# A four-layer graph network on one core: the sage layer of one graph beside the second layer's sums of the next

## Time and profile before

| | us |
|---|---|
| median of 3 runs | 9451.15 |
| the profiled execution | 9428.1 |
| its span | 9426.5 |
| busy in it: PE / DVE / ACT / POOL | 5518.7 / 6030.4 / 4617.4 / 5142.9 |
| mean granted TensorE clock | 0.796 |

### The profile page before, as it was taken

How to read it: one execution, slowest core, us unless ns; L and a number is a source line. 1 busy time by engine, 2 the same in 40 slices (tenths; PEclk the granted TensorE clock), 3 DMA queues, 4 the chain that set the end, 5 groups by cost and what they waited for, 6 DMA issues and landing times.

```text
span 9426.5 us, 190384 instructions
## 1 busy us (share of the span) xinstructions
PE 5518.7 (59%) x62584; PEld 4902.9 (52%) x62584; DVE 6030.4 (64%) x7458; ACT 4617.4 (49%) x4674; POOL 5142.9 (55%) x5234
## 2 busy tenths in 40 slices
PE   3673771266765567466775667564774668563036
PEld 2663771254765467364764557463773548462025
DVE  5874872276866677586866777585875768573024
ACT  5643740355726466265735566254744567261034
POOL 0004777677727676276726774276744777176720
PEclk9886885688888789787887889787886789786568
DMA  2114332334313523234313432125322343223210
GB/s 95 42 33 108 71 69 31 55 79 93 74 47 61 121 58 77 51 65 108 67 45 73 116 65 68 46 47 130 60 59 62 85 84 73 65 42 72 26 22 28
DMA packets 305351, 629.20 MB, mean 67 GB/s; under 512 B 113273, under 2 KB 163962, under 8 KB 268666
## 3 DMA queue, kind: packets, MB, share of 16 engines
q0 software_dynamic: 91936, 161.87, 16.1%
q1 hardware_dynamic: 207922, 456.31, 13.8%
q10 hardware_dynamic: 4752, 0.14, 0.0%
HBM read 506.89 MB, written 111.15 MB: 66 GB/s over the span
## 4 chain that ended last, share of the span: by engine, by line
DVE 28%; PE 22%; issue 13%; ACT 7%; POOL 4%; DVEq 3%; DMA 2%; ACTq 2%; POOLq 0%; SPq 0%
PE ps L1318 6%; DVE keys L1063 4%; PE ps L1293 3%; PE ps L1320 3%; PE ps L1343 3%; DVE key L1053 3%; ACT Pbuf L690 3%; PE ps L1274 2%; PE ps L1271 2%; ACT Hn L690 2%; PE ps L1367 2%; DVE Hn L923 2%; DMA G<-table,idx 2%; DVE key L1039 2%; DVE Zs L943 1%
## 5 line engine op out<-in xcount | busy, mean ns | idle before, releaser
L541 POOL DMA_INDIRECT G<-table,idx x1416 | 1502.3, 1061 | 510.0 <-issue 448.9
L1320 PE MATMUL ps<-Hn,AT 128*128 128x99 bf16 x12288 | 1763.4, 216 | 0.0
L533 POOL DMA_DIRECT2D idx<-lists x433 | 260.0, 600 | 2731.1 <-issue 2246.7
L1320 PE MATMUL ps<-X,AT 128*128 128x99 bf16 x12288 | 1739.9, 215 | 0.0
L690 ACT ACTIVATE Hn<-Rb,q 128x2048 int8<-128x2048 f32 x768 | 1484.1, 1987 | 66.9 <-PE ps L1320 63.9
L690 ACT ACTIVATE Pbuf<-Rb,q 128x2048 int8<-128x2048 f32 x768 | 1487.2, 1987 | 17.7 <-PE ps L1320 15.4
L541 POOL DMA_INDIRECT best<-table,idx x1024 | 1102.7, 1077 | 321.8 <-issue 309.4
L1318 PE MATMUL ps<-X,Hn 128*128 128x198 bf16 x6144 | 939.5, 269 | 554.1 <-DVE Hn L923 304.2
L1320 PEld LDWEIGHTS ps<-Hn,AT 128*128 128x128 fp8e4 x12288 | 1252.1, 102 | 0.0
L1320 PEld LDWEIGHTS ps<-X,AT 128*128 128x128 fp8e4 x12288 | 1245.9, 101 | 0.0
L1318 PE MATMUL ps<-Hn 128*128 128x198 bf16 x6144 | 950.5, 270 | 430.8 <-DVE Zs L943 241.5
(11 more groups left out here) (186 smaller groups left out, 11651.5 us busy)
## 6 DMA issues: line engine op xcount, KB each, us to landing
Rb<-in_adj SPq DMA_DIRECT2D x128, 1024.0 KB
Rb<-rrows SPq DMA_DIRECT2D x104, 1024.0 KB, 6.4
bytes_A<-A SPq DMA_DIRECT2D x128, 256.0 KB
bytes_AT<-AT SPq DMA_DIRECT2D x128, 256.0 KB
AT<-bytes_AT SPq DMA_DIRECT2D x128, 256.0 KB, 3.4
AT<-bytes_A SPq DMA_DIRECT2D x128, 256.0 KB, 3.4
G<-table,idx POOLq DMA_INDIRECT x1416
h<-Hn SPq DMA_DIRECT2D x16, 1024.0 KB, 4.2
```

The costliest lines, as they stand in the source:

```text
L533: pool.dma_start(idx[:, slot, :], lists[bass.ds(r, 1)].rearrange("o p k -> (o p) k")).then_inc(idx_in[slot], 16)
L541: pool.indirect_dma_start(out=dst[:, k, :], out_offset=None, in_=table, in_offset=bass.IndirectOffsetOnAxis(ap=idx[:, slot, k:k + 1], axis ...
L1320: ins = pe.matmul(both[:, 0, 0:G], A8[:, jb, at], v[:, 0:G], start=False, stop=jb == T - 1, skip_group_check=True)
```

## The change

The sage layer of graph b moves from behind LB of graph b+1 to beside its sums. TensorE works on it after a key block's matmuls: after block 1 it waits for gather b and for h1, x1; after blocks 1 to 8 it transposes two tiles into bank 6, after blocks 2 to 9 it does the products of two tiles into bank 7. ScalarE copies a pair of tiles at once and does norms 4 and 2 ahead of LB's Exp and norm 1. VectorE adds the bias to pair p after weighing block p+4 and takes its statistics after block p+5; gamma, beta, relu, the sum into X2 and statistics 2 (`joined`) stand between the last block and `finish`. The three parts of tile 8's list stand after blocks 0, 1 and 2, and SyncE stores them. E of `finish` and WH of LC move to other places of their buffers. For graph 0's LB there is nothing beside, and the last graph's sage layer runs alone.

```diff
             load(0, True)
-            first(0, True)
+            heads_of(0, True)
+            beside(0, None)
...
                 with eng.Fori(0, B - 2) as b:
-                    second(b, False)
+                    beside(b + 1, b)
+                    middle(b, False)
                     last_layer(b, b + 2, False)
-                    first(b + 2, False)
+                    heads_of(b + 2, False)
...
# SyncE, beside
+            def beside(b, other):
+                if b is None:
+                    restore(other + 1, other)
+                    return
                 exponentials(LB, 1, b)
                 sp.dma_start(Rb[:, 0, :], rrows[1, 0, :].partition_broadcast(P)).then_inc(S[LB]["rin0"], 16)
+                if other is not None:
+                    store_lists(b, LIST_LB)
...
# ScalarE
+            def sage_operands(b):
+                s = M["sage"]
+                with act.Fori(0, T // 2) as tt:
+                    plain(act)
+                    act.wait_ge(s["T"], b * T + tt * 2 + 2)
+                    act.wait_ge(s["W"], b * T + tt * 2 + 2)
+                    act.activation(hT[:, :, :, :], ps[:, 6, :].rearrange("p (u k c) -> p u k c", u=2, k=2),
+                                   ACT.Copy).then_inc(s["hT"], 2)
...
+            def beside(b, other):
+                if b is not None:
+                    prepare(LB, b)
+                if other is not None:
+                    sage_operands(other)
+                    norm(4, other, Y, Y, ACT.Identity)
+                    norm(2, other, X2, Hn2, ACT.Relu)
+                if b is not None:
+                    elu_exp(LB, b, 0)
+                    norm(1, b, X, Hn, ACT.Relu)
...
# VectorE
+            def sage_sums(b, p):
+                plain(dve)
+                dve.wait_ge(M["sage"]["W"], b * T + (2 * p + 4))
+                dve.tensor_tensor(Y[:, 2 * p:2 * p + 2, :], ps[:, 7, 0:2 * F].rearrange("p (t f) -> p t f", t=2),
+                                  rowsb[:, 0:1, :].broadcast_to([P, 2, F]), ALU.add).then_inc(M["sage"]["ev"], 2)
+            def sage_statistics(b, p):
+                plain(dve)
+                dve.wait_ge(M["sage"]["ev"], b * T + (2 * p + 4))
+                for t in (2 * p, 2 * p + 1):
+                    dve.bn_stats(stats[:, t, :], Y[:, t, :]).then_inc(ln[4]["st"], 1)
+            def beside(b, other):
+                rest_of = []
+                between = [] if other is None or b is None else list(zip((0, 1, 2), list_tile(b, LIST_LB)))
+                if other is not None:
+                    for p in range(T // 2):
+                        between.append((p + 4, lambda p=p: sage_sums(other, p)))
+                        between.append((p + 5, lambda p=p: sage_statistics(other, p)))
+                    between.append((T // 2 + 4, lambda: rest_of.append(deviations(4, other))))
+                    between.append((T // 2 + 5, lambda: rest_of[0]()))
...
+                    prepare(LB, b)
+                    weigh(LB, 0, (b + 1) * 16, slice(0, 1), b, between)
+                if other is not None:
+                    joined(other)
+                if b is not None:
+                    finish(LB, b, lone)
+                    statistics(1, b, X)
...
# TensorE
+            def sage_step(b, jb):
+                if jb == 1:
+                    sage_arrived(b)
+                if 2 <= jb < T // 2 + 2:
+                    sage_product(b, jb - 2)
+                if 1 <= jb < T // 2 + 1:
+                    sage_turned(b, jb - 1)
...
+            def sums(L, hn, other):
...
                     ins.then_inc(s["pe"], 1)
+                    if other is not None:
+                        sage_step(other, jb)
```

More of the change, by code:

```diff
@@ L385, in load, with heads_of @@
                         sp.dma_start(stage_i32[:, u, :], src).then_inc(adj_in[u], 16)
-            def first(b, alone):
+            def heads_of(b, alone):
                 plain(sp)
@@ L455, in restore, with middle @@
                 sp.dma_start(flat(X2), of(x1, after - 1)).then_inc(x1_in, 16)
-            def second(b, alone):
-                if alone:
-                    restore(b + 1, b)
+            def middle(b, alone):
                 with sp.Fori(0, T) as t:
@@ L489, in _ @@
             sp.sem_inc(out_done, 16)
-            pipeline(sp, load, first, second, last_layer)
+            pipeline(sp, load, heads_of, beside, middle, last_layer)
             sp.wait_ge(out_done, B * 16 + 16)
@@ L814, in _ @@
             act.wait_ge(ready, 1)
-            pipeline(act, load, first, second, last_layer)
+            pipeline(act, load, heads_of, beside, middle, last_layer)
         @block.vector
@@ L825, in statistics, with moments, deviations @@
                                  src[:, bass.ds(t, 1), :].rearrange("p o c -> p (o c)")).then_inc(ln[k]["st"], 1)
+                moments(k, b)
+            def moments(k, b):
+                deviations(k, b)()
+            def deviations(k, b):
                 plain(dve)
@@ L834, in statistics, with inverse @@
                 v(dve.tensor_tensor(small[:, 4, :], small[:, 4, :], small[:, 3, :], ALU.add))
[L836 to L840, removed]
+                def inverse():
+                    plain(dve)
+                    dve.wait_ge(ln[k]["root"], b + 1)
+                    v(dve.reciprocal(small[:, 0, :], small[:, 4, :]))
+                    v(dve.scalar_tensor_tensor(small[:, 1, :], small[:, 2, :], -0.5, small[:, 0, :], ALU.mult, ALU.mult))
+                    v.end()
+                return inverse
             def prepare(L, b):
@@ L885, in weigh @@
             def weigh(L, slot, loaded, h, hn, between=()):
-                after = dict(between)
                 s = S[L]
@@ L896, in weigh @@
                                              ALU.max, ALU.mult).then_inc(s["p"], 1)
-                    if jb in after:
-                        after[jb]()
+                    for at, work in between:
+                        if at == jb:
+                            work()
             def split(L, m, h, u, k):
@@ L1161, in first @@
                 heads(LA, b, lone, (b, *(LIST_ALL if alone else LIST_LA)))
[L1162 to L1176, removed]
-                plain(dve)
-                dve.wait_ge(M["sage"]["ev"], (b + 1) * T + 2)
-                statistics(4, b, Y)
+            def sage_sums(b, p):
+                plain(dve)
+                dve.wait_ge(M["sage"]["W"], b * T + (2 * p + 4))
+                dve.tensor_tensor(Y[:, 2 * p:2 * p + 2, :], ps[:, 7, 0:2 * F].rearrange("p (t f) -> p t f", t=2),
+                                  rowsb[:, 0:1, :].broadcast_to([P, 2, F]), ALU.add).then_inc(M["sage"]["ev"], 2)
@@ new lines, in sage_statistics @@
+            def sage_statistics(b, p):
[12 more added lines that the diff above has]
+                    between.append((T // 2 + 5, lambda: rest_of[0]()))
+                if b is None:
+                    for at, work in sorted(between, key=lambda part: part[0]):
+                        work()
+                else:
+                    prepare(LB, b)
[5 more added lines that the diff above has]
+                    statistics(1, b, X)
@@ L1180, in second, with joined @@
+            def joined(b):
                 v = Chain(dve, M["sage"]["y"], b * 3, 3)
@@ L1237, in last_layer, with prepare @@
                 dve.tensor_tensor(X2[:, :, :], X2[:, :, :], Y, ALU.add).then_inc(x_done, 1)
-            pipeline(dve, load, first, second, last_layer)
+            pipeline(dve, load, heads_of, beside, middle, last_layer)
         @block.tensor
         def _(pe):
-            def prepare(L, b, source, arrived):
+            def prepare(L, b, source, arrived, alone=False):
                 s, w = S[L], Wf[L]
                 W = L.H * L.D + 2 * L.H
-                if not arrived:
+                if L is LB:
                     plain(pe)
                     pe.wait_ge(S[LA]["pv"], ((b + 1) * LA.H + 2) * POST[LA])
+                if L is LC:
+                    plain(pe)
+                    pe.wait_ge(S[LB]["pv"], (b + (2 if alone else 3)) * POST[LB] + 3)
                 for tt in range(T // 2):
@@ L1282, in prepare, with sage_turned, sage_product, sage_arrived @@
                 pe.matmul(ps[:, 6, 0:L.H * L.C], ones[:, :], hpart[:, 0:L.H * L.C], start=True, stop=True).then_inc(s["hs"], 1)
-            def sums(L, hn):
+            def sage_turned(b, p):
+                s = M["sage"]
+                plain(pe)
+                pe.wait_ge(s["hT"], b * T + (2 * p + 2))
+                for u in range(2):
+                    pe.transpose(ps[:, 6, 2 * u * P:(2 * u + 1) * P], Hn2[:, 2 * p + u, :], ident[:, :])
+                    ins = pe.transpose(ps[:, 6, (2 * u + 1) * P:(2 * u + 2) * P], Agg[:, 2 * p + u, :], ident[:, :])
+                ins.then_inc(s["T"], 2)
+            def sage_product(b, p):
+                s = M["sage"]
+                plain(pe)
+                pe.wait_ge(s["hT"], b * T + (2 * p + 4))
```

(24 more changed lines are left out.)

18 lines of the change are left out of this document (10 added, 8 removed).

## The result

The changed kernel takes 9320.38 us (median of 4 runs, 9293.71 to 9324.41) against 9456.33 for the kernel before in the same comparison: ratio 0.9855, 95% interval [0.9833, 0.9877], 136 us less. Two later comparisons gave 0.9841 [0.9819, 0.9863] and 0.9853 [0.9827, 0.9879]. The direction was right, but the gain is nearly double the 72 us that I had forecast, and 9320 lies under my range (9335 to 9450). The profiled execution took 9293.71 (span 9292.0), 134 us under the one before.

A forecast was written before the change was run, and what follows sets the result against it. No engine binds; order and waits set the time. Terms +58 + 189 - 323 + 13 = -63, gather 7 -4, tail about -5: together -72, so 9451 - 72 = 9379 us (profiled execution 9356), range 9335 to 9450.

The forecast's parts named there:

- Rivals 1: Gathers take 2% longer beside denser work, 18 us each, replacing the sage layer as bound: 9435 us, no change; chance 0.14.
- rival 2: Sums of seven LB stages: TensorE's clock stays 0.50 through blocks 3 to 9, +206 us, 9585, slower; chance 0.10.
- the list's pause: TensorE stands still after blocks 0 to 2 for tile 8's list; some 8 us with two rounds, clock loss +2.5.
- Rival 3: More hidden than counted: LB stages grow by 22 us each, checked by gathers 1, 5 and 6: 9346 us; chance 0.14.
- Graph 0: Graph 1's LB stops after block 1 until gather 0 ends at 1741.1; LC(0)'s first hT copy at 1861: +58 us.
- Six LB stages: Graphs 2 to 7, first weighing to LC: three stages at 30.1 and three at 32.8 us longer, +189 us.
- a wait of +13: Graph 3's LB, block 1: TensorE waits 20 us for gather 2, hiding the list's pause and clock loss; +13 remain.
- Gather 7: Last gather: follows norm 1 of graph 7 by 12.0 instead of 16.4 us, -4, and takes 828.4 us again.
- My Theory A: Rerun's forecast: gather 0 933 us as VectorE stands still, gather 7 815 as sage 6 leaves its first tiles.
- The removed stretches, 5 x 64.6: Passes of LC(1) to LC(5): LC's first hT copy follows norm 1 at once, 64.6 us less each, -323 us.
- the tail: After gather 7: the last sage layer stands alone with its statistics between the pairs, about -5 us.

The follow-up runs named there:

- the wait alone: The kernel before with one edit: TensorE waits after key block 1 of LB for the gather of the graph before; 9528.5 us, ratio 1.009.
- second and third executions: The changed kernel run again twice, unchanged, in the first and the last of three comparisons; medians 9303.3 and 9303.2 us.
- late `joined`: The changed kernel with `joined` behind statistics 1 and norm 2 behind norm 1 in every LB with a sage layer; run twice, 9275.5 and 9270.2 us.
- the kernel with its loop turned round: The changed kernel with graph 0's sage layer alone after gather 0, not beside graph 1's LB, which turned the loop's order round; 9325.6 us, ratio 0.986.

## Why the prediction was off

Its mechanism held step by step. LC's first copy follows norm 1 within 0.1 us. From the first weighing, the last one ended after 71.5 to 74.0 us (one round) and 79.2 to 81.8 (two) against 73 and 81.2 forecast, and `finish` began after 90.9 to 93.5 and 98.5 to 101.1 against 93.6 and 101.6. TensorE stood 320.6 us at gather 0 (340 forecast) and met gather 2, for which I had forecast 20 us, and gather 5, which I had given 5 us of room. Gather 1 started at 1853 (1873 forecast), gather 7 at 8094 (8145). Rivals 1 and 2 did not occur: gathers 0 and 7 became shorter, not 2% longer, and the pace of the blocks was 4.9 us. In graph 5's pass the granted clock was 0.50 in the list's pause (5863.6 to 5873.8) and 1.00 from 5874 to 5930, with TensorE busy 53.2 of 56 us. What I took from the Trainium skill for rival 2 stands on its page "TensorE: Matmul & The Clock Gate" under "A second HAM failure mode: psum-queue depth-cycling", right behind the section that I named; these rows hold no such short stops and do not test it. Rival 3 had the direction, but for another reason: the LB stages grew by 24.9 to 32.8 us each, not by its 22, so that its 9346 lies nearer to the result is luck. By the profiled execution three terms of the sum were mis-sized, and one held:

- **Graph 0: forecast +58, measured +38** (1841.3 against 1803.1; 1838 and 1840 in the other two executions). 14 of the 20 are gather 0's end. I took its length as given, "everything up to the end of gather 0" outside the edit, while the edit empties VectorE beside it. This is the step that failed in kind, and the wait alone showed it. In the prediction I had written down that GpSimd stretches VectorE's small steps, and did not turn the sentence round.
- **Six LB stages: forecast +189 and a wait of +13, measured +168 together.** The waits for gathers 2 and 5 (7.6 and 5.9 us) hid in the list's pause and cost 1 to 3. The five stages inside the loop took 3 to 6 us less than forecast each, the last one, outside it, 3 more. Most of this lies between `finish` and norm 1's end, 35.6 us for a forecast 38.1: the table load that I put before the Exp fell beside VectorE's steps (L677 at 5949.32), and the next one, for norm 1's Sqrt, ran ahead of its wait instead of behind it (L630 at 5952.54), so that statistics 1 and norm 1 took 17.8 us for 19.6. In the last LB both loads stood behind their waits, and statistics 1 and norm 1 took 19.9. Up to the last weighing the pace of the steps (4.9 us for 5.07) gave some 1 us. The clock's loss after the pause was some 2 us with two rounds for a forecast 2.5 (in graph 5's pass 6.08 us between two weighings, against 4.08 in graph 4's, where the clock did not fall), and 1.5 in graphs 2 and 7 with one round, for which I had forecast none. In the second and third executions, with longer waits, these six stages cost +197 and +188, so that much of this term's miss belongs to the first execution.
- **Gather 7: taken as 828.4 again, measured 815** (812 to 820 in every order with the overlap, 829 with the wait alone, 823 with the sage layer after the sums). Its cause is not settled. My Theory A named sage 6's part beside its first tiles, but late `joined` stands there too with 814 to 817, and in the changed kernel the first tile got longer, not shorter (54 against 47 us). By its Agg copies the sixth tile took 41 instead of 55 us and the eighth and ninth 4 less each; which VectorE work is beside them differs, but that was not tested.
- **The removed stretches, 5 x 64.6, held:** from LC's first copy to the next LB the six stages sum to 5445 us before and 5446 after. Over the profiled executions of all kernels this sum lies anywhere from 5374 to 5455. In the two executions of the first kernel with `joined` late it differs by 59 us, of the 73 between their totals.

The three misses are 20, 34 and 13 us. The profiled execution lies 62 us under its forecast 9356; small terms the other way (the six stages between, the tail) took the other 5.

The drain of about 1380 ns that the Trainium skill ("ScalarE: Activation LUTs", "What ACT_TABLE_LOAD costs") puts on top of a switch is not in the trace: L677's load of 1.28 us at 5949.32 is followed by the Exp at 5950.61.

That the result lies outside the range is also the range's fault. I had all the bounds at the stages and none at the two gathers, of 1777 us together, that stand on the path with no slack.

## What to carry to other kernels

A stage on the critical path that the edit doesn't touch is not a constant: ask what runs beside it, and whether the edit empties or fills that engine. Here GpSimd's gather 0 got 16 to 20 us shorter when VectorE stood still beside its end, and was 14 to 28 us longer than that when the same work stood beside it again. Moving work beside a bound matrix stage paid only through the interleaving, block by block; the same order without it gained nothing. After such a change look again for the wait that is next: writing the table before `joined`, so that the gathers start earlier, gave another 33 us.

## What the runs showed of the hardware

- GpSimd's TENSOR_SCALAR on 128x512 f32 took 614 ns alone and 2046 ns beside VectorE's weighing of two SBUF operands; an indirect DMA's issue 949 and 1472 ns. A gather of 929 to 933 us with 19 to 39 us of VectorE's work beside its end was 947 to 961 with 62 to 94 us of it.
- A table load on ScalarE may run ahead of the wait of the instruction that needs it (5952.54, inside the changed kernel's loop) or behind it (its first and last LB, outside the loop; the loop of the kernel before; the kernel with its loop turned round). With it behind the wait, the stretch from statistics 1 to norm 1's end was 1.6 to 2.1 us longer. What decides between the two was not tested.
